# Retention and local attention in one kernel: the keys' first product ahead of the states, the last slot of the retention reordered, and GpSimd's bias between root and rotated sums

## The reference

```python
# block 3, retention: 8 heads of 32 channels, gammas per head
qT, kT, vT = (proj(Wq), proj(Wk), proj(Wv))
S = g * S + k_t[..., :, None] * v_t[..., None, :]
y_t = jnp.einsum('bhde,bhd->bhe', S, q_t)
...
out = (out - mean) * jax.lax.rsqrt(var + EPS)      # per head, over time
out = out.reshape(B, L, D) * gn_weight + gn_bias
return out @ Wo.T
```

```python
# block 4, one of two layers
q, k, v = jnp.split(shift_token(x) @ wqkv, 3, axis=-1)
q, k = l2norm(q) * qs, l2norm(k) * ksc
q, k = rotary_xpos(q, k)
x = x + local_attention(q, k, v) @ wo              # windows of 128 tokens
h = layernorm(shift_token(x)) * lg + lb
a, g = jnp.split(h @ w1 + b1, 2, axis=-1)
x = x + (a * gelu(g)) @ w2 + b2
```

## Time and profile before

| what | us |
|---|---|
| median of 3 runs | 2361.08 |
| lowest, highest | 2354.46, 2362.95 |
| the profiled execution, its own time | 2357.87 |
| its span, first to last instruction | 2356.1 |
| PE busy in the span | 2254.7 |
| DVE, ACT, POOL busy | 1639.4, 1254.6, 731.8 |

### The profile page before, as it was taken

One profiled execution on the slowest core, in us unless ns is written; L12 is line 12 of the kernel. 1 busy time (PEld: TensorE's weight loads), 2 busy tenths in 40 slices (PEclk: granted clock), 3 DMA queues, 4 the chain that ended last, 5 costly groups with the idle time before them and its releaser, 6 DMA issues.

```text
span 2356.1 us, 42487 instructions
## 1 busy us (share of the span) xinstructions
PE 2254.7 (96%) x16306; PEld 1322.2 (56%) x16306; DVE 1639.4 (70%) x4252; ACT 1254.6 (53%) x2823; POOL 731.8 (31%) x730
## 2 busy tenths in 40 slices
PE   8999999999898989988899999999999999999998
PEld 3333333333632867765566666666666666666665
DVE  6788888886510846667876777677767777787764
ACT  4666666665221532237666556556665666566640
POOL 3343233321020411134433333343333333333321
PEclk7999999999998999999999999999999999999999
DMA  7444333334279020000000000000001000000001
GB/s 237 144 148 118 118 118 114 117 105 164 94 321 396 2 90 19 19 28 21 6 6 6 1 6 6 6 1 32 15 5 53 6 15 22 13 14 23 21 23 39
DMA packets 68617, 158.44 MB, mean 67 GB/s; under 512 B 6256, under 2 KB 49120, under 8 KB 63936
## 3 DMA queue, kind: packets, MB, share of 16 engines
q1 hardware_dynamic: 65856, 146.55, 17.5%
q0 software_dynamic: 2560, 9.18, 1.7%
HBM read 116.39 MB, written 35.13 MB: 64 GB/s over the span
## 4 chain that ended last, share of the span: by engine, by line
PE 74%; DVE 15%; ACT 4%; DMA 3%; issue 2%; POOL 1%; SPq 0%; POOLq 0%; DVEq 0%; ACTq 0%
PE banks L2046 10%; PE banks L2024 7%; PE banks L1905 6%; PE banks L1919 5%; PE banks L232 5%; PE banks L272 4%; PE banks L245 4%; PE banks L2006 3%; PE banks L1949 3%; PE banks L1964 3%; DVE arena L481 2%; DVE arena L2589 2%; PE banks L1931 2%; DMA arena<-in_e_Wg 2%; PE banks L1428 1%
## 5 line engine op out<-in xcount | busy, mean ns | idle before, releaser
L481 DVE TENSOR_REDUCE arena<-banks 128x1 f32<-128x512 f32 x512 | 323.4, 681 | 72.1 <-PE banks L232 72.0
L393 ACT ACTIVATE arena<-banks 128x512 f32<-128x512 f32 x512 | 280.2, 595 | 146.3 <-PE banks L245 144.2
L2046 PE MATMUL banks<-arena 128*128 128x512 f32 x640 | 293.2, 594 | 1.0 <-DVE arena L2231 1.0
L2128 ACT ACTIVATE arena<-arena 128x256 f32<-128x256 f32 (+1 forms) x512 | 286.5, 562 | 5.0 <-DVE arena L2237 4.5
L2384 POOL TENSOR_TENSOR arena<-arena 128x512 f32<-128x512 f32 x128 | 162.7, 1271 | 380.0 <-DVE arena L2268 380.0
L1905 PE MATMUL banks<-arena 128*128 128x512 f32 x512 | 241.5, 594 | 2.8 <-DVE arena L2268 2.8
L232 PE MATMUL banks<-arena 96*128 96x512 bf16 x512 | 204.8, 403 | 17.5 <-DVE arena L481 14.3
L245 PE MATMUL banks<-arena 128*128 128x512 bf16 x512 | 195.0, 387 | 2.8 <-ACT arena L393 2.2
L2380 POOL TENSOR_TENSOR arena<-arena 128x16 f32<-128x16 f32 x64 | 189.4, 2959 | 5.3
L2100 ACT ACTIVATE arena<-arena 128x256 f32<-128x256 f32 (+1 forms) x256 | 102.1, 471 | 163.2 <-DVE arena L2213 163.2
L2046 PEld LDWEIGHTS banks<-arena 128*128 128x128 f32 x640 | 115.5, 190 | 126.7 <-issue 116.5
(11 more groups left out here) (302 smaller groups left out, 4238.1 us busy)
## 6 DMA issues: line engine op xcount, KB each, us to landing
arena<-in_e_W SPq DMA_DIRECT2D x16, 2048.0 KB, 16.2
arena<-stacks SPq DMA_DIRECT2D x64, 384.0 KB, 4.5
arena<-in_e_Wg SPq DMA_DIRECT2D x8, 2048.0 KB, 17.8
stacks<-arena SPq DMA_DIRECT2D x32, 384.0 KB, 2.5
stacks<-arena SPq DMA_DIRECT2D x32, 256.0 KB, 2.8
arena<-dens POOLq DMA_DIRECT2D x32, 256.0 KB, 4.6
arena<-in_xT SPq DMA_DIRECT2D x8, 512.0 KB, 7.9
stacks<-arena SPq DMA_DIRECT2D x32, 128.0 KB, 2.5
```

The lines of the kernel that those rows point to most:

```text
L393: e.activation(ex[:, j], self.psum[:, self.exp_bank1(k)], ACT.Exp).then_inc(s["a_e"], 1)
L481: e.tensor_reduce(split(self.maxima[n % 2][:, 0:16], TILES, UNIT)[:, t, j:j + 1], self.psum[:, k % 3], AX.X, ALU.max, negate=True).then_in ...
L2046: i = e.matmul(bank, weights[:, c], self.hT[:, c], start=c == 0, stop=c == 1)
L2128: k = e.activation(pr[:, h, at:], pr[:, h, at:], ACT.Exp, bias=mx[:, h:h + 1], scale=rn[:, h:h + 1], accum_out=den[:, h:h + 1])
```

## The change

Four moves, and nothing is added or left out. In `tensor3_slot` the first key product of unit a is issued before the two states of unit b. In the last slot of block 3 VectorE makes the coefficients of unit b-1 before the state masks and masks the scores of half 1 before the sums of half 0. In slot 2 of block 4 ScalarE copies the first turned half of unit 6 before it divides tile 0's weights. On GpSimd the bias goes from behind the tile's work to between the root and the rotated sums; where a slot has no tile any more, it stays where it was.

```diff
@@ tensor3_slot
         if b is not None:
+            if a is not None:
+                self.tensor3_project(e, w, "k", a, 0)
             self.tensor3_state(e, w, b, 0)
             self.tensor3_state(e, w, b, 1)
+        elif a is not None:
+            self.tensor3_project(e, w, "k", a, 0)
         if a is not None:
-            self.tensor3_project(e, w, "k", a, 0)
             self.tensor3_project(e, w, "k", a, 1)
@@ vector3
         self.vector3_own(e, w, b, 0)
+        self.vector3_coefficients(e, w, b - 1)
         self.vector3_state(e, w, b, 0)
         self.vector3_state(e, w, b, 1)
-        self.vector3_coefficients(e, w, b - 1)
         self.vector4_lengths(e, w, 0)
+        self.vector3_own(e, w, b, 1)
         self.vector3_sums(e, w, b, 0)
-        self.vector3_own(e, w, b, 1)
@@ scalar4
+            if n == 2:
+                self.scalar3_turn(e, w, SEQS - 2, 0)
             if c is not None:
                 self.scalar4_divide(e, w, c)
-            if n == 2:
-                self.scalar3_turn(e, w, SEQS - 2, 0)
@@ gpsimd4
             if n < TILES4:
                 self.gpsimd4_tile(e, w, n)
+            else:
+                self.gpsimd4_bias(e, w, n)
             self.gpsimd4_mlp(e, w, n)
@@ gpsimd4_mlp
-            elif r == 1:
-                w.wait_ge("m_shifted", 32 * (m + 1))
-                w.wait_ge("m_half", 2 * m + 2)
-                w.wait_ge("m_norm", m + 1)
-                w.wait_ge("l_late", 16)
-                e.tensor_tensor(x, x, repeated(self.S(f"b_2{l}"), TILES), ALU.add).then_inc(s["m_bias"], 1)
+    def gpsimd4_bias(self, e, w, slot):
+        for m in range(MLPS):
+            l, b = divmod(m, SEQS)
+            if slot == MLP_STEP * m + MLP_FIRST + 1:
+                x = self.x_nat[:, b]
+                w.wait_ge("m_shifted", 32 * (m + 1))
+                w.wait_ge("m_half", 2 * m + 2)
+                w.wait_ge("m_norm", m + 1)
+                w.wait_ge("l_late", 16)
+                e.tensor_tensor(x, x, repeated(self.S(f"b_2{l}"), TILES), ALU.add).then_inc(self.s["m_bias"], 1)
```

## The result

The changed kernel takes 2369.16 us (median of 6 runs, 2368.32 to 2371.27) against 2353.86 us for the kernel before (6 runs, 2350.32 to 2362.95). The ratio is 1.0061, 95% interval 1.0045 to 1.0077, so it is 10.6 to 18.1 us slower on 2353.86; 2377.9 was forecast, +16.8 on the 2361.08 that was known then. The profiled execution took 2368.32 us, its span 2366.5.

The account below looks back on a forecast made before the run. PE was taken to bound the kernel, busy 2254.7 of 2356.1 us. Terms +20.5 - 1.0 - 2.2 + 0 - 0.5 = +16.8 us gave 2377.9 on the median 2361.08; own range 2372 to 2386, stated range down to 2357.

Parts of the forecast that it names:

- One sign of the list: Block 4's bias slots: PE would idle 1.3 to 1.6 us before the transposed weights, released by VectorE's maxima.
- The bias: Block 4, m = 1 to 13: moved bias delays a small VectorE operation 1.98 us, stalling PE 1.58 a slot; +20.5 us.
- what PE has in hand before w1: Slack before PE's second transposed-weights step in block 4, put at 0.40 us and subtracted from VectorE's 1.98 us delay.
- rival (a): Block 4: the small VectorE operation comes first or isn't held, so no stall; -3.7 us, 2357.4; chance 0.20.
- (b): Block 4: PE has more in hand, stall only 0.3 to 1.0 us a slot; 2361 to 2370 us; chance 0.13.
- (c): All holes filled count in full and the bias is harmless; -9.4 us, 2351.7; chance 0.05.
- Slot 8: First bias slot of block 4 (m = 0), order of bias and small operation uncertain; -1.0 us, bounds 0 and -2.2.
- Some 1.2 stay: At m = 0, if the small operation wins, some 1.2 of the 2.13 us saved at the keys' scaling remain.
- The keys' product: Block 3, slots 1 to 7: hole before the states filled, head-norm wait takes most back; -2.2 us, bounds 0 and -6.3.
- The last slot: Last slot of block 3: earlier coefficients and scores before sums win nothing; 0, bounds -0.1 and +0.3 us.
- the turn: Block 4, ACT's copy ahead of the division fills its 1.01 us idle time; -0.5 us, bounds 0 and -0.9.
- "slower": Whole kernel slower by over 0.5%, above 2372.9 us; chance 0.61.

Follow-up runs that it names:

- the bias behind the first operation: Changed kernel with GpSimd's bias waiting for the first of the slot's two small VectorE operations; 2346.72 us in one run.
- early coefficients: Changed kernel with the bias waiting for both small VectorE operations, plus block 3's head-norm coefficients before the state masks in every slot; 2343.17 us, ratio 0.9948.
- all but the bias: Changed kernel with the bias put back behind the rotated sums; 2352.68 us, 0.9988 of the kernel before.
- the key product alone: Kernel before with only the first key product moved ahead of the states in block 3; 2352.10 us in one run.
- the bias behind both small operations: Changed kernel with GpSimd's bias waiting until both small VectorE operations of the slot are done; 2350.69 us, 0.9989 of the kernel before.
- the bias alone: Kernel before with only GpSimd's bias moved between root and rotated sums; 2373.8 us, ratio 1.0085.

## Why the prediction was right

The direction, the mechanism and nearly the size came out, and each term can be set beside its row. One sign of the list came out low: PE's idle time before the transposed weights is 1.23 us, where 1.3 to 1.6 was written, since part of the stall shows as later starts inside the group.

**The bias.** Forecast: the small operation 1.98 us late, the stall 1.58 a slot, 20.5 us in 13 slots. Measured: 1.99 late, 1.68 a slot, 21.8. The term that was slightly mis-sized is what PE has in hand before w1: 0.31 us, not 0.40. The rest of the step held as written: who is held, who is not, that s2 and s3 are what PE waits for, that the keys' scaling gains as much as is lost and that PE gets nothing for it. Only the run with the bias behind the first operation shows how near rival (a) was: with the same bias starting 0.24 us after that operation starts, instead of 0.22 before it, the 13 slots cost nothing.

The rule of the Trainium skill, SBUF — State Buffer, section "SBUF: two separate sides", says the same as these runs: the pair of ports goes to whoever starts first, for the whole instruction, and a VectorE operation with two SBUF operands needs it against a GpSimd operation that reads SBUF. The trace agrees: 2.15, 1.07 and 1.06 us for an operation of 0.16, each ending with GpSimd's, and an unchanged 0.68 us for those behind them that read PSUM.

The other rivals: (b), a stall of 0.3 to 1.0 us a slot, is out by the 1.68; (c), that all holes count, by the six waits for the head norm.

**Slot 8.** Forecast -1.0 between 0 and -2.2, measured -2.2. As thought, the first small operation won and the second was held. "Some 1.2 stay" was close for what it priced: PE's stall of 2.29 us is down to 0.18, 2.11 less, and the second small operation, 0.77 us longer, takes that much back, which is the 1.34 between roots 8 and 9 (18.01 to 16.67). What the term had left out is the other 0.84 us, between roots 9 and 10 (15.82 to 14.98): the stall had been followed by slow matmuls; see the last section.

**The keys' product.** Forecast -2.2, measured -1.95 from the products of slot 1 to y of the last slot: 1.0 in slot 1, which has no gate, where 0.75 was forecast; 0.15 to 0.22 in each of slots 2 to 7, where 0.24 was forecast; and 0.12 lost again on the way into the last slot. The gate was named and is there, and the run with early coefficients shows it to be the cause.

**The last slot** 0 and **the turn** -0.5: as forecast, the second with the reservation above.

**The sum.** +16.8 forecast, +17.4 by the parts of the trace, +14.4 (10.6 to 18.1) by the runs. The absolute time was forecast 8.7 us too high; 7.2 of these are the base, 2361.08 in three runs and 2353.86 in the six beside the changed kernel. Of the shares, "slower" had 0.61, and the interval lies on both sides of 0.5%. The measured 2369.16 is also below 2372, the lower edge of the forecast's own range, and inside the stated one only because that reaches down to rival (a). The base did this and not the mechanism: on 2353.86 the same sum gives 2365 to 2379.

What stays open: why the first 830 us, the same code in both kernels, differ by 5.5 us between the two profiled executions.

## What to carry to other kernels

Before moving a large GpSimd operation into a gap of its own engine, list the VectorE operations that will run beside it and mark those with two operands in SBUF, however small: an operation of 0.16 us on 128x4 numbers was made 1.99 us longer, where the one on 128x512 had been made 2.13 longer, and it stood ahead of what TensorE waited for. A stretched operation in a profile is only worth moving if someone waits for it; the 2.1 us by which the old place stretched VectorE's scaling in each of 13 slots, some 28 us, had cost the kernel nothing (20.76 us with it and without it).

And where a hole is filled by reordering, ask what was just behind. Here it was a head norm, and on top of the reorder three tiny operations moved ahead of two masks gave 5.0 us (164.58 to 159.57), where the reorder itself had given 1.95.

## What the runs showed of the hardware

**The clock after a stall.** Behind the stall of 2.29 us in slot 8 the kernel before runs at half clock for about 3.4 us, which is 1.2 GHz of 2.4 (from:to, us, busy of each engine, granted clock, DMA):

```profile
1164.00:1167.00 3.00, 1.14 (x16) 1.00 (x20) 2.96 (x7) 1.14 (x3) 1.17 (x1) 0.90 0.00 0
1167.00:1170.00 3.00, 3.00 (x88) 3.00 (x82) 1.93 (x5) 2.61 (x6) 0.07 (x1) 0.53 0.00 0
1170.00:1173.00 3.00, 3.00 (x24) 1.82 (x18) 2.79 (x20) 0.58 (x2) 2.92 (x2) 1.00 0.02 5
```

The three kernels whose profile has this stall (before, all but the bias, the key product alone) all have the dip, and the six in which that stall is gone (0.18 us is left of it in the changed kernel) don't. So removing 2.1 us of idle time gave 2.96 us in the kernel with the bias behind both operations (18.01 + 15.82 to 15.90 + 14.97). The other 0.85 can be read on PE. From the product that ended the stall to the next value product it takes 1170.40 - 1165.86 = 4.54 us with the dip, and 1162.30 - 1158.61 = 3.69 without it. The start of the first is in the earlier trace rows; the other three starts, the kernel before first:

```profile
1170.40 1.98 PE L1919 MATMUL banks<-arena 128*128 128x512 f32 x4
```

```profile
1158.61 0.63 PE L1934 MATMUL banks<-arena 128*128 128x128 f32 x4 [0.17 <-DVE arena L2279]
...
1162.30 1.98 PE L1922 MATMUL banks<-arena 128*128 128x512 f32 x4 [0.35 <-ACT arena L2081]
```

**The same stall, with and without a dip.** In the last slot of block 3 PE waits 2.70 us for VectorE's masked scores in all nine kernels. In four of nine profiles (before, the bias alone, the bias behind both, the early coefficients) a dip of the same length follows, and the interval from root 0 to root 1 is 20.57 to 20.78 us; in the other five it is 19.16 or 19.17. This is the -1.5 of the third row of the table above. Windows of the two profiles there, before first:

```profile
1038.00:1041.00 3.00, 3.00 (x41) 2.35 (x41) 0.62 (x2) 0.05 (x1) 1.27 (x1) 0.65 0.00 0
```

```profile
1031.00:1034.00 3.00, 3.00 (x37) 2.60 (x29) 2.93 (x8) 0.60 (x1) 1.27 (x1) 1.00 0.00 0
```

Equal idle time, equal work, another clock: one profile of a kernel is not enough to credit such a difference to a change. What decides whether a dip follows, no run here shows.
